# Two-layer graph network on one core: 64-byte-aligned matmul operands, and the projections' low parts subtracted by VectorE instead of GpSimd

## What is computed

```
h = relu(layernorm(x))
for layer in (0, 1):
    u    = h @ h.T / sqrt(384)
    a    = softmax(u, axis=-1);  delta = a * adj
    attn = delta / (sum(delta, -1) + 1e-10)
    hl, hs, hr = h @ wl.T + bl,  h @ ws.T + bs,  h @ wr.T + br
    ctx  = (attn * upper) @ hl + diag(attn) * hs + (attn * lower) @ hr
    h    = relu(layernorm(ctx) * g + beta)
out = x + h
```

## Time and profile before

| | |
|---|---|
| median of three runs | 1225.69 us |
| profiled execution: time, span | 1223.43 us, 1221.7 us |
| granted TensorE clock, mean | 0.996 |
| busy: PE, DVE, ACT, POOL | 1204.9, 914.9, 514.8, 537.9 us |
| chain that ended last | PE 96%, DVE 2%, issue 1% |

### The profile page before, as it was taken

How to read it: one execution, slowest core, us unless ns; L and a number is a source line. 1 busy time by engine, 2 the same in 40 slices (tenths; PEclk the granted TensorE clock), 3 DMA queues, 4 the chain that set the end, 5 groups by cost and what they waited for, 6 DMA issues and landing times.

```text
span 1221.7 us, 18789 instructions
## 1 busy us (share of the span) xinstructions
PE 1204.9 (99%) x7146; PEld 1184.1 (97%) x7146; DVE 914.9 (75%) x2046; ACT 514.8 (42%) x1061; POOL 537.9 (44%) x614
## 2 busy tenths in 40 slices
PE   9999999999999999999999999999999999999996
PEld 7899999999999999999999999999999999999995
DVE  6567994679955898558985599755997568966688
ACT  4345433355333453344443434435343453435441
POOL 4364343454524444334444254442454434444334
PEclk9999999999999999999999999999999999999998
DMA  8001320013200131001310023100221003210000
GB/s 301 20 21 40 107 78 1 1 61 96 69 2 1 61 113 53 1 1 61 112 53 1 1 68 106 53 1 1 90 84 53 1 3 110 71 42 1 1 27 27
DMA packets 37002, 60.85 MB, mean 50 GB/s; under 512 B 2352, under 2 KB 27952, under 8 KB 36912
## 3 DMA queue, kind: packets, MB, share of 16 engines
q1 hardware_dynamic: 36624, 59.26, 14.9%
q10 hardware_dynamic: 288, 0.39, 0.1%
HBM read 47.06 MB, written 12.58 MB: 49 GB/s over the span
## 4 chain that ended last, share of the span: by engine, by line
PE 96%; DVE 2%; issue 1%; POOL 0%; ACT 0%; DMA 0%; POOLq 0%; DVEq 0%
PE rot_ps L271 16%; PE rot_ps L272 16%; PE rot_ps L273 16%; PE u_ps L271 14%; PE u_ps L272 14%; PE u_ps L273 14%; PE rot_ps L337 3%; PE u_ps L329 1%; PE rot_ps L346 1%; DVE et_lo L619 0%; ACT x_norm L416 0%; DVE x_stats L556 0%; DMA x_norm<-x_dram 0%; POOL rstd L893 0%; DVE z L684 0%
## 5 line engine op out<-in xcount | busy, mean ns | idle before, releaser
L876 POOL TENSOR_TENSOR hw_lo<-proj,hw_hi 128x384 fp32r<-128x384 f32 x256 | 260.9, 1036 | 332.9 <-ACT hw_hi L468 332.9
L271 PE MATMUL rot_ps<-w_hi,ht_hi 128*128 128x384 f32 x1152 | 392.5, 341 | 0.8 <-DVE proj L647 0.8
L272 PE MATMUL rot_ps<-w_lo,ht_hi 128*128 128x384 f32 x1152 | 388.3, 337 | 0.0
L273 PE MATMUL rot_ps<-w_hi,ht_lo 128*128 128x384 f32 x1152 | 388.0, 337 | 0.0
L271 PEld LDWEIGHTS rot_ps<-w_hi,ht_hi 128*128 128x128 f32 x1152 | 216.4, 188 | 1.1 <-DVE proj L647 1.1
L272 PEld LDWEIGHTS rot_ps<-w_lo,ht_hi 128*128 128x128 f32 x1152 | 216.5, 188 | 0.0
L273 PEld LDWEIGHTS rot_ps<-w_hi,ht_lo 128*128 128x128 f32 x1152 | 216.2, 188 | 0.0
L441 ACT ACTIVATE u_off<-u_ps 128x384 f32<-128x384 f32 x64 | 28.0, 438 | 364.2 <-PE u_ps L273 364.2
L647 DVE TENSOR_TENSOR proj<-rot_ps,bias 128x384 f32<-128x384 f32 x256 | 138.3, 550 | 52.5 <-PE rot_ps L273 52.4
L888 POOL TENSOR_TENSOR dg<-et_hi,tri 128x256 fp32r<-128x256 f32 x128 | 103.5, 809 | 140.9 <-PE u_ps L273 140.9
L468 ACT ACTIVATE hw_hi<-proj 128x384 fp32r<-128x384 f32 x256 | 125.8, 519 | 82.5 <-DVE proj L647 82.4
(11 more groups left out here) (88 smaller groups left out, 2047.1 us busy)
## 6 DMA issues: line engine op xcount, KB each, us to landing
out_dram<-z SPq DMA_DIRECT2D x64, 192.0 KB, 1.9
x_norm<-x_dram SPq DMA_DIRECT2D x15, 768.0 KB, 4.5
adj_a<-adj_t_dram SPq DMA_DIRECT2D x8, 1024.0 KB, 5.4
adj_b<-adj_t_dram SPq DMA_DIRECT2D x8, 1024.0 KB, 5.5
x_a<-x_dram SPq DMA_DIRECT2D x8, 768.0 KB, 4.6
x_b<-x_dram SPq DMA_DIRECT2D x8, 768.0 KB, 4.9
w_stage<-w_t_dram SPq DMA_DIRECT2D x4, 576.0 KB, 5.3
e_sb<-w_t_dram SPq DMA_DIRECT2D x1, 576.0 KB, 4.9
```

The costliest lines, as they stand in the source:

```text
L271: pe.matmul(dst, a_hi, b_hi, start=first and m == 0, stop=False)
L272: pe.matmul(dst, a_hi, b_lo, start=False, stop=False)
L273: done = pe.matmul(dst, a_lo, b_hi, start=False, stop=last and m == n - 1)
L876: pool.tensor_tensor(hw_lo[:, t, n, 0:dim], proj[:, t % 2, n, :], hw_hi[:, t, n, 0:dim].bitcast(F32), ALU.subtract).then_inc(hw_lo_done, 1)
```

## The change

The kernel's SBUF declarations are put into another order, with the matmul operands first and the small tensors last, and rows of `hw_hi` become 400 elements long (a multiple of 64 bytes) while rows of `hw_lo` shrink to 384. The product hi x lo is made for the columns of the low part only, 384 instead of 386. `proj_low` moves from GpSimd's queue to VectorE's, whose order is written out anew for both layers. ScalarE's order stays as it is. GpSimd keeps the ones, the triangles and the roots, and sets two constants fewer.

```diff
+    LINE = 64
+    HW_ROW = -(-EXT * 4 // LINE) * (LINE // 4)
...
-        ident = sb("ident", [P, P])
-        tri = sb("tri", [P, 2, P])
-        minus_half = sb("minus_half", [P, TILES])
+
         w_hi = sb("w_hi", [P, layers, KB, 3 * dim], F32R)
         w_lo = sb("w_lo", [P, layers, KB, 3 * dim], F32R)
+        ht_hi = sb("ht_hi", [P, 2, KB, n_rows], F32R)
+        ht_lo = sb("ht_lo", [P, 2, KB, n_rows], F32R)
+        et_hi = sb("et_hi", [P, TILES, n_rows], F32R)
+        et_lo = sb("et_lo", [P, TILES, n_rows], F32R)
+        hw_hi = sb("hw_hi", [P, TILES, 2, HW_ROW], F32R)
+        hw_lo = sb("hw_lo", [P, TILES, 2, dim], F32R)
+        dg = sb("dg", [P, 2, 2, 2, P], F32R)
...
-                    pe.matmul(dst, a_hi, b_lo, start=False, stop=False)
+                    pe.matmul(dst[:, 0:b_lo.shape[1]], a_hi, b_lo, start=False, stop=False)
...
-                                        hw_hi[:, j, n, :], hw_lo[:, j, n, :])], first=m == 0, last=False)
+                                        hw_hi[:, j, n, 0:EXT], hw_lo[:, j, n, :])], first=m == 0, last=False)
...
+                def proj_low(t, n):
+                    dve.wait_ge(hw_hi_done, at(it, s, 2 * t + (n + 1), EIGHT))
+                    dve.tensor_tensor(hw_lo[:, t, n, :], proj[:, t % 2, n, :], hw_hi[:, t, n, 0:dim].bitcast(F32),
+                                      ALU.subtract).then_inc(hw_lo_done, 1)
...
                 if layer == 0:
                     mask(0)
                     evacuate(0, 0)
                     evacuate(0, 1)
                     mask(1)
+                    proj_low(0, 0)
                     mask(2)
+                    proj_low(0, 1)
                     evacuate(1, 0)
                     mask(3)
                     e_low(0)
                     evacuate(1, 1)
+                    proj_low(1, 0)
                     e_low(1)
                     e_low(2)
+                    proj_low(1, 1)
                     evacuate(2, 0)
...
                     e_low(3)
+                    evacuate(2, 1)
+                    proj_low(2, 0)
...
                     diagonal(0)
-                    evacuate(2, 1)
...
+                    diagonal(1)
...
+                    evacuate(3, 0)
+                    proj_low(2, 1)
                     diagonal(2)
                     diagonal(3)
+                    evacuate(3, 1)
...
+                    evacuate(0, 2)
+                    proj_low(3, 0)
+                    evacuate(1, 2)
+                    proj_low(3, 1)
+                    evacuate(2, 2)
+                    evacuate(3, 2)
                 else:
...
                     evacuate(1, 0)
                     evacuate(1, 1)
+                    proj_low(0, 0)
+                    proj_low(0, 1)
                     shift_scores(0)
                     shift_scores(1)
                     evacuate(2, 0)
                     shift_scores(2)
+                    proj_low(1, 0)
                     shift_scores(3)
+                    proj_low(1, 1)
                     mask(0)
                     evacuate(2, 1)
                     mask(1)
+                    proj_low(2, 0)
                     mask(2)
...
+                    evacuate(3, 0)
+                    proj_low(2, 1)
                     mask(3)
                     e_low(0)
+                    evacuate(3, 1)
                     e_low(1)
                     evacuate(0, 2)
+                    proj_low(3, 0)
                     e_low(2)
                     evacuate(1, 2)
+                    proj_low(3, 1)
                     evacuate(2, 2)
                     e_low(3)
                     evacuate(3, 2)
...
-                proj_low(0)
                 set_ones()
-                proj_low(1)
-                if s < 2:
-                    triangles(0)
-                    proj_low(2)
-                    if first and s == 0:
-                        x_rstd_of(2)
-                    triangles(1)
-                    proj_low(3)
-                else:
-                    proj_low(2)
-                    proj_low(3)
-                    triangles(0)
-                    triangles(1)
+                if first and s == 0:
+                    x_rstd_of(2)
+                triangles(0)
+                triangles(1)
```

## The result

The changed kernel takes 1282.5 us (median of five runs, 1280.68 to 1284.05) against 1225.31 us for the kernel before on the same chip: ratio 1.0468, interval 1.0453 to 1.0482. Its profiled execution takes 1282.5 us with a span of 1280.7 us, 59.0 us more than before. The forecast was 1275 us, with a range of 1222 to 1284. That range is wide enough to hold the time of no change too; the forecast case's own range was 1266 to 1282, and the measured time is 0.5 us beyond it.

The account below looks back on a forecast made before the run. TensorE's matmuls were taken as the bound. 1223.4 us plus 52.5 (the move) minus 1.9 (384 columns) gave 1274.0, less 1 relief 1273, plus 2.3 from profiled execution to median 1275; range 1222 to 1284, own 1266 to 1282.

Parts of the forecast that it names:

- forecast case: Steps s = 2 and 3 (layer 1): VectorE's queue sets their length, matmul spacing unchanged; 1275 us, chance 0.46.
- VectorE idle ahead of low part (2,0): Layer 1, step s = 3: VectorE's in-order queue stands idle 2.4 us until ScalarE delivers hw_hi of (2,0).
- delays of the turns of h: Step s = 3, TensorE's turn of h for db = 1: late VectorE evacuations cost 1.2 us, then 0.5 us more.
- s = 3 longer by: Layer 1, steps s = 3: attend(0) starts later and TensorE cannot recover it; 3.9 us a step, seven steps.
- s = 2 longer by: Layer 1, steps s = 2: same queues without two x_norm instructions, idle 1.2 us; 2.8 us a step, eight steps.
- Layer 0's cover: Layer 0, evacuation (2,0) before unit (0,2): 1.94 us slack hides four low parts of 1.88 us; zero cost taken.
- The relief: VectorE's et_lo, without GpSimd low parts beside it, gets 1 to 2 us a step back; 1 us off the total.
- D: Layer 1: VectorE regains more than it gives, no stalls, TensorE still bounds; 35 us gained, 1190 us, chance 0.15.
- B: VectorE's queue stalls layer 1, but alignment shortens each of 164 matmuls a step by 6.7 ns; 1250 us, chance 0.20.
- C: VectorE's queue stalls layer 1, but alignment shortens each of 164 matmuls a step by 12 ns; 1238 us, chance 0.12.
- E: Whole kernel: the cover over VectorE's added work holds and alignment gives nothing; 1224 us, chance 0.07.
- the one that named VectorE's longest wait: Sign of being right: VectorE's longest wait is low part (2,0) for ScalarE's hw_hi, near 2.4 us in s = 3.

Follow-up runs that it names:

- edit 1: Low parts moved from GpSimd to VectorE in the changed order, old layout and 386-column products, against the kernel before: 1284.69 us, ratio 1.0491.
- Edit 2: New operand layout, row lengths and 384-column low product, both queues as in the kernel before, against that kernel: 1220.87 us, ratio 0.9966.
- the wait shortened: Changed kernel with ScalarE's first two x_normalise placed behind round_proj(2) in steps s = 3: 1272.41 us, ratio 1.0386 to the kernel before.

## Why the prediction was right, and where it was not

**The forecast case held**, in mechanism and in place, and not by luck in its numbers: the single delays came within 0.2 us of the forecast. The time itself was 7.5 us off, from terms that the sum did not have. Point by point, with the delays as they are in the step s = 3:

| step of the prediction | forecast | measured |
|---|---|---|
| VectorE idle ahead of low part (2,0) | 2.4 us | 2.32 us |
| delay of unit (2,2) | 1.5 us | 1.44 us |
| delay of unit (3,2) | 0.6 us | 0.44 us |
| delays of the turns of h | 1.2 and 0.5 us | 1.40 and 0.44 us |
| s = 3 longer by | 3.9 us | 4.18 us |
| s = 2 longer by | 2.8 us | 2.96 us |
| VectorE time of a low part | 552 ns | 604 ns mean, 557 without triangles |
| layer 0 | no stall | none after the first pair; 1.22 us in the second step |

A measured delay is the start of the unit less the start that the pace before it would have given, 311.15 - 309.54 - 0.17 for (2,2). The 52.5 us of edit 1 were 23.7 + 29.3 us in those 15 steps and 3.8 us in the last, where `attend(0)` starts 29.85 us into the step and not 26.04: 56.8. The step s = 3 is longer by what was not in its sum: the four delays come to 3.7 us of the forecast 3.8, the four restarts add some 0.3 us, and `attend(0)` starts at 318.32, right behind `et_lo(3)` (317.59 + 0.68 = 318.27) and some 0.2 us after the last turn would have let it. The last step was taken as an s = 2 with 2.8 us, and has a wait of its own, 3.2 us for `et_lo` ahead of `attend(0)`. Order rather than work makes nearly all of it: the same work elsewhere in the queue costs 9.3 us.

**Layer 0's cover held, just.** Of the 1.94 us between the evacuation and the unit in the kernel before, in s = 1, I meant four low parts to use up 1.88. The tightest place turned out to be s = 0: evacuation (2,0) ends at 191.38 and unit (0,2) starts at 191.53 (VectorE's and TensorE's timeline):

```profile
190.83 0.55 DVE L655 TENSOR_TENSOR proj<-rot_ps,bias 128x384 f32<-128x384 f32 x1
```

```profile
191.53 0.34 PE L274 MATMUL rot_ps<-w_hi,ht_hi 128*128 128x384 f32 x1
```

**Edit 2 was mis-stated.** "What is sure is that `hw_lo` is read with 384 and not 386 columns: -1.9 us" failed: that edit alone is worth nothing. The 177 and 174 ns compared matmuls of `attend` with projections, and put their whole difference down to two columns. The rows had a better price: 128 columns make 229 - 176 = 53 ns of the scores' pace, so two columns are an estimated 0.8 ns and 640 matmuls 0.5 us, and scores of 384 columns already stood at 176 ns. The alignment, taken at zero, is worth zero. And the layout gave 4.1 us by a cause that was not in my list, the place of `ht` or of what moved with it. The trace of before has a hint of it, a step s = 0 of 37.34 beside s = 1 of 37.04 us with TensorE bound in both, and I had read only s = 1, 2 and 3. The size was off by 2 us.

**The relief was put in the wrong terms.** I expected `et_lo` at 0.68 to 1.0 us; its mean fell only from 947 to 863 ns, and single ones take 1.21 us. With the triangles cut the mean is 681 ns, so the triangles took the place of the low parts beside it. What they cost on the path is 11.8 us in the fifteen full steps of layer 1 by the run with the triangles cut, and the forecast had only part of that, in `et_lo(1)`. The 1 us taken off for the relief no run shows by itself.

**What was missing:** the half-clock stretches, 3.0 us in two steps and 1.8 us in the last (its 5.6 us less the 3.8 of stalls; with the wait shortened the last step's `attend(0)` starts as late, there is no stretch of 6.83 us, and it is 1.8 us shorter), and the second step's 1.5 us beside `w_lo`. On the profiled executions the forecast was +49.6 and the measurement +59.1 us. The gap is 4.3 (edit 1) + 4.8 (half clock) + 1.5 (second step) - 1.0 (steps s = 0 gave 3.9, 1.4 of it in the first step alone, where edit 2 and the relief were to give 2.9) = 9.6 us, the 9.5 us to rounding. The forecast's 2.3 us from profiled execution to median did not come again, since the profiled execution of the changed kernel is its median: that leaves the 7.5 us, again to rounding.

**Rivals.** D (no stalls) is refuted: TensorE waits 37.3 us for `hs` and `proj`. B and C are refuted as spacing: projections are 173 ns apart, not under 170, and edit 2 alone gives 4.2 us and not 24 or 36. E is refuted by layer 1. Of the signs, the one that named VectorE's longest wait was too strong: its wait for `hw_hi`, at most 2.3 us, is the new one, but a wait for TensorE before an evacuation reaches 3.5 us.

## What to carry to other kernels

Before a cheap instruction moves to another in-order queue, ask what it waits for and what stands behind it there: here 0.5 us of work stood in front of an evacuation and cost 3 to 4 us, and the same work placed behind the evacuations cost a sixth of it. Follow the stalls to the engine that sets the end, add up to 0.1 us for each restart, and look for half-clock stretches once TensorE is no longer busy throughout. Compare steps with equal instruction counts in the trace: a difference between them points at a pace that no instruction's own row shows, and one trace of a kernel need not have it in the steps where another has it.

## What the runs showed of the hardware that I had not expected

- Once TensorE stalls by 1 to 3 us a step, stretches of 3.41 us at a granted clock of 0.50 (1.2 GHz) appear in some of the steps: two in the changed kernel's steps s = 2, three in the run with the wait shortened, one in the run with low part (2,0) behind the masks (and one more in its last step); none before the last step in the kernel before, nor in the run of the move alone or the one with the triangles cut, although these two stall as well. Each adds 1.5 us to its step. Steps of the same stalls mostly have none, and the mean granted clock of the changed kernel's five executions lies between 0.992 and 0.995; what picks them is open.
- The pace of the projections' 384-column matmuls was 177 or 173 ns with no wait in the trace, and the slower one never came in layer 0, behind the first pair, once `ht` lay behind `w_lo`. The Trainium skill (SBUF — State Buffer, section "Who interferes with whom") says that TensorE reads weights and the moving operand through ports of their own and never waits on anyone; no wait for another engine shows here either, and yet the placement is worth 4 us a run. What in the reads makes it, no run here shows.
- A start at a multiple of 64 bytes, rows that are multiples of 64, and two columns fewer in one of three products: nothing in sum each (1220.52 against 1220.87 us, and ratios 1.0006 and 1.0000).
- VectorE's `et_lo` of 0.68 us took 2.70 us beside one GpSimd instruction of 2.99 us, and a `diagonal` of 0.28 us took 2.74 us beside one of 2.65 us.
